# A new order of the prologue of a butterfly FFN kernel, on all engines at once

## The reference, cut to what matters

```python
# x, ctx: (32, 512, 512) f32; 16384 tokens of 512 values
def xattn(q, k, v):                       # k = v = ctx
    r_t = 0.9 * r_{t-1} + k_t * v_t       # along the 512 steps of a batch
    return q * r_t
def ffn(x):
    h = x @ W_exp + b_exp                 # 512 -> 2048
    h = butterfly(h, up_weights)          # 11 stages of 2x2 blocks; stage s pairs i and i + 2**s
    h = gelu(h + up_bias)
    h = butterfly(h, down_weights)
    return h @ W_con + b_con + down_bias  # 2048 -> 512
x = x + xattn(layernorm(x), ctx, ctx)
x = x + ffn(layernorm(x))
```

## Time and profile before

| | us |
|---|---|
| median of three runs | 2770.97 |
| the profiled execution | 2771.06 |
| its span, first to last instruction | 2769.2 |
| first 160 us | the prologue |
| TensorE busy | 2740.1 (99%) |
| VectorE busy | 2122.9 (77%) |
| ScalarE busy | 1131.0 (41%) |
| GpSimd busy | 396.5 (14%) |

### The profile page before, as it was taken

How to read it: one execution, slowest core, us unless ns; L and a number is a source line. 1 busy time by engine, 2 the same in 40 slices (tenths; PEclk the granted TensorE clock), 3 DMA queues, 4 the chain that set the end, 5 groups by cost and what they waited for, 6 DMA issues and landing times.

```text
span 2769.2 us, 35072 instructions
## 1 busy us (share of the span) xinstructions
PE 2740.1 (99%) x12191; PEld 2260.4 (82%) x12191; DVE 2122.9 (77%) x3554; ACT 1131.0 (41%) x1715; POOL 396.5 (14%) x561
## 2 busy tenths in 40 slices
PE   8899999999999999999999999999999999999998
PEld 6778888888888888888888888888888888888887
DVE  9878787778878777787877878787787877778533
ACT  5743434334343433434343343434434343343432
POOL 4712011110201111010110101011020111102000
PEclk8999999999999999999999999999999999999999
DMA  9795765758576575856757585675857557584543
GB/s 275 266 294 152 216 191 167 228 154 240 165 204 203 168 213 155 255 163 195 201 170 223 155 239 168 190 214 162 235 152 224 185 175 223 161 243 152 182 149 99
DMA packets 292021, 540.48 MB, mean 195 GB/s; under 512 B 36918, under 2 KB 98518, under 8 KB 274950
## 3 DMA queue, kind: packets, MB, share of 16 engines
q1 hardware_dynamic: 285456, 535.77, 64.7%
q10 hardware_dynamic: 5414, 1.25, 0.3%
q0 software_dynamic: 976, 1.22, 0.2%
HBM read 445.83 MB, written 60.82 MB: 183 GB/s over the span
## 4 chain that ended last, share of the span: by engine, by line
PE 98%; ACT 1%; issue 0%; DVE 0%; DMA 0%; ACTq 0%
PE ps L1767 44%; PE ps L1788 25%; PE ps L1801 25%; PE ps L1664 1%; PE ps L1570 1%; PE ps L1642 0%; PE ps L1668 0%; ACT wcon L863 0%; PE ps L1662 0%; ACT w1r L885 0%; PE ps L1670 0%; PE ps L1868 0%; DMA wexp<-in_L_ffn_W_exp_dram 0%; PE ps L1716 0%; PE ps L1589 0%
## 5 line engine op out<-in xcount | busy, mean ns | idle before, releaser
L1767 PE MATMUL ps<-xop,w1r 128*128 128x512 f32 x5376 | 1364.1, 389 | 2.5 <-DVE xop L1296 1.6
L1767 PEld LDWEIGHTS ps<-xop,w1r 128*128 128x128 f32 x5376 | 1008.8, 188 | 212.7 <-DVE xop L1296 2.0
L1788 PE MATMUL ps<-w2r,ghi 128*128 128x512 f32 x2048 | 630.5, 389 | 0.0
L1801 PE MATMUL ps<-w2r,ghi 128*128 128x512 f32 x2032 | 625.8, 389 | 0.0
L1002 ACT ACTIVATE st<-ps 128x512 f32<-128x512 f32 x384 | 229.7, 598 | 839.9 <-PE ps L1767 839.9
L1403 DVE TENSOR_TENSOR x<-ps,x 128x512 f32<-128x512 f32 x508 | 348.6, 686 | 280.6 <-PE ps L1801 278.2
L1788 PEld LDWEIGHTS ps<-w2r,ghi 128*128 128x128 f32 x2048 | 384.4, 188 | 79.8
L1801 PEld LDWEIGHTS ps<-w2r,ghi 128*128 128x128 f32 x2032 | 381.2, 188 | 79.8 <-DVE glo L1426 0.4
L1421 DVE TENSOR_TENSOR g<-ps,st 128x512 f32<-128x512 f32 x384 | 262.9, 685 | 212.5 <-PE ps L1767 212.1
L1006 ACT ACTIVATE g<-g,gelu_bias 128x512 f32<-128x512 f32 x384 | 275.4, 717 | 362.7 <-DVE g L1421 361.6
L1426 DVE TENSOR_TENSOR glo<-g,ghi 128x512 fp32r<-128x512 f32 x510 | 347.5, 702 | 79.9 <-ACT ghi L1020 79.8
(11 more groups left out here) (174 smaller groups left out, 1701.8 us busy)
## 6 DMA issues: line engine op xcount, KB each, us to landing
w1r<-w_products SPq DMA_DIRECT2D x889, 256.0 KB, 3.3
w2r<-w_split SPq DMA_DIRECT2D x126, 1024.0 KB, 5.0
x<-in_x_dram SPq DMA_DIRECT2D x128, 256.0 KB, 7.2
raw<-kv SPq DMA_DIRECT2D x480, 64.0 KB, 2.2
out_dram<-x SPq DMA_DIRECT2D x120, 256.0 KB, 4.0
kv<-in_ctx_dram SPq DMA_DIRECT2D x64, 256.0 KB, 7.3
raw<-in_ctx_dram SPq DMA_DIRECT2D x64, 256.0 KB, 5.3
wexp<-in_L_ffn_W_exp_dram SPq DMA_DIRECT2D x4, 1024.0 KB, 10.9
```

Source lines behind the costliest of these rows:

```text
L1767: last = nc.tensor.matmul(bank[:, :], w1r[:, slot, w, c * P:(c + 1) * P], xop[:, XPOS[m], v, c, :], start=(opens and i == 0), stop=(i == l ...
L1788: last = nc.tensor.matmul(ps_ya[j][:, :], g[:, p % 2, q, j * P:(j + 1) * P], w2r[:, p % 2, kk, w, :], start=(p == 0 and kk == 0 and i == 0 ...
L1801: last = nc.tensor.matmul(ps_yb[:, :], g[:, p % 2, q, j * P:(j + 1) * P], w2r[:, p % 2, kk, w, :], start=(kk == 0 and i == 0), stop=(kk == ...
```

## The change

It reorders the prologue on all five engines. Nothing after the first `product` is changed.

Loads: the two `PARTED` up stages are now loaded by SyncE, ahead of W_exp; the 15 small up loads of the high stages come ahead of the context rows; the last quarter of W_exp comes behind the context rows. The second half of x is loaded after `Z`, the second half of the context beside the `low_up` stores; `Z` comes back in five parts.

The rest of the diff, cut:

```diff
@@ fold steps
-                        last = nc.tensor.matmul(o, LX[:, 1, 4 * i + c, :], rank_major(ident[:, :]), start=True, stop=True)
+                        last = nc.tensor.transpose(o, LX[:, 1, 4 * i + c, :], ident[:, :])
-                return LX[:, 1, 4 * i:4 * i + 4, :].rearrange("p a b -> p (a b)"), whole
+                return LX[:, 1, 4 * i:4 * i + 4, :].rearrange("p a (r e) -> p a r e", e=E),\
+                    whole.rearrange("p (a e r) -> p a r e", a=4, e=E)
+                if kind == "bias_low":
+                    wait_kept(pe, "bcol", 0)
+                    for k in range(KH):
+                        last = nc.tensor.matmul(bank[:, k:k + 1], LX[:, 0, k, :], bcol[:, k:k + 1], start=True, stop=True)
@@ TensorE, high_dn
-            pe.wait_ge(bcol_kept, 1)
-            for k in range(KH):
-                last = nc.tensor.matmul(ps[4][:, 256 + k:257 + k], LX[:, 0, k, :], bcol[:, k:k + 1], start=True, stop=True)
                 fold_step("high_dn", r)
+                if r == 3:
+                    fold_step("bias_low", 0)
@@ TensorE, behind the tokens
-            pe.wait_ge(low_matrix_ready, 2)
-            for q in range(KH // 4):
-                fold_step("turn_low", q)
@@ ScalarE
+            for lane in (0, Q):
+                act.activation(sel_parts[lane:lane + Q], part_choice[0:Q], ACT.Copy).then_inc(sel_rounded, 1)
+            for stage in PARTED:
+                coefs_hi(0, stage)
+            for k in range(3):
+                fold_step("WT", k)
+            top_hi(0)
+            act.wait_ge(top_sel_ready, 2)
+            for lane in (0, Q):
+                act.activation(top_sel[lane:lane + Q], top_choice[0:Q], ACT.Copy).then_inc(top_sel_ready, 1)
+            for k in range(3, 8):
+                fold_step("WT", k)
+            coefs_hi(1, PARTED[0])
+            for k in range(8, 12):
                 fold_step("WT", k)
             for k in range(KH):
                 fold_step("low_up", k)
+                if k in WT_LAST:
+                    fold_step("WT", WT_LAST[k])
                 if k == 1:
+                    coefs_hi(1, PARTED[1])
+                if k == 3:
                     square(0, 0)
             top_hi(1)
-            act.wait_ge(path_product, UP_DONE)
-            act.wait_ge(mask_ready, 1)
-            for e in range(E):
-                last = act.activation(HX[:, 0, :, :]...)          # line 931
+            square(0, 1)
...
             for q in range(R // 4):
                 fold_step("turn_high", q)
+            for q in range(KH // 4):
+                fold_step("turn_low", q)
             weights_hi(0)
@@ VectorE
             lane_rows(0)
             coefs_lo(0)
             low_products(0)              # top_lo(0) now inside, ahead of stage 4
             top_products(0)
+            (the memsets of decay and keep, and the sum same_e)
             lane_rows(1)
             coefs_lo(1)
-            for j in range(J):
-                scan_chunk(0, 0, j)
-            stats1(0, 0, xs[0], range(J))
-            high_products(0)
+            scan_chunk(0, 0, 0)
+            scan_chunk(0, 0, 1)
+            high_products(0)
+            scan_chunk(0, 0, 2)
+            stats1(0, 0, xs[0], range(J))
+            scan_chunk(0, 0, 3)
+            gate(0, 0, xs[0], 0)
+            gate(0, 0, xs[0], 1)
+            low_products(1)
+            high_products(1)
+            top_lo(1)
+            gate(0, 0, xs[0], 2)
+            gate(0, 0, xs[0], 3)
+            top_products(1)
             dve.wait_ge(mean1_ready, J)
             stats1(0, 1, xs[0], range(J), means=False)
-            for j in range(J):
-                gate(0, 0, xs[0], j)
             means1(1)
-            top_lo(1)
-            low_products(1)
-            high_products(1)
             for j in range(J):
                 normalise(0, 0, xs[0], j)
-            top_products(1)
             scan_chunk(1, 1, 0)
             scan_chunk(1, 1, 1)
+            weights_lo(0)
             scan_chunk(1, 1, 2)
-            weights_lo(0)
             weights_lo(1)
@@ GpSimd
+            high_matrix(0)
+            pool.wait_ge(fold_made, fold_at("low_up", 11) + 1)
+            nc.gpsimd.memset(top_parts[1].bitcast(f32), 0.0).then_inc(top_zeroed, 1)
             rstd_rows(0)
-            rstd_gated(0)
+            rstd_gated(0, (0, 1))
+            high_matrix(1)
+            rstd_gated(0, (2, 3))
             rstd_rows(1)
-            pool.wait_ge(xn_ready, J)
-            high_matrix(1)
```

More of the change, by code:

```diff
@@ L250, in xattn_ffn_program @@
         up_stored = sem("up_stored")
-        z_loaded = [sem(f"z_loaded{q}") for q in range(4)]
+        z_loaded = [sem(f"z_loaded{q}") for q in range(len(Z_PARTS) - 1)]
         w1_hi = sem("w1_hi")
@@ L318, in xattn_ffn_program @@
         FOLD += [("tokens", i, "act") for i in range(2, J)]
-        FOLD += [("turn_low", q, "act") for q in range(KH // 4)]
         FOLD += [("back", k, "act") for k in range(10)]
@@ L404, in kept @@
             if kind == "low_up":
-                return low_folded[:, i, :], whole
+                return Z[:, i, :], whole
+            if kind == "bcol":
+                return bcol, whole[:, 0:2 * KH]
+            if kind == "bias_low":
+                return yb, whole[:, 0:KH]
             if kind == "high_up":
@@ L952, in _ @@
             weights_hi(1)
-            for r in range(3, 8):
+            fold_step("high_dn", 3)
+            fold_step("bias_low", 0)
+            for r in range(4, 8):
                 fold_step("high_dn", r)
@@ L959, in _ @@
             fold_step("high_dn", 12)
+            for group in range(2):
+                act.wait_ge(w1_stored[0][group], NX)
             for i in range(2):
@@ L1120, in path_products @@
                     bank, col = places[stage]
+                    if stage == PARTED[0] and not dn and not first:
+                        top_lo(0)
                     dve.wait_ge(coef_spread, spread_count(dn, first + max(stage, PARTED[0] - 1)))
@@ L1644, in fold_step @@
                     return
+                if kind == "bcol":
+                    pe.wait_ge(bias_rows_loaded, 2 * NX)
+                    nc.tensor.transpose(bank[:, 0:2 * KH], bias_rows, ident[0:2 * KH, 0:2 * KH]).then_inc(fold_made, 1)
+                    return
+                if kind == "bias_low":
+                    wait_kept(pe, "bcol", 0)
+                    for k in range(KH):
+                        last = nc.tensor.matmul(bank[:, k:k + 1], LX[:, 0, k, :], bcol[:, k:k + 1], start=True, stop=True)
+                    last.then_inc(fold_made, 1)
+                    return
                 if kind == "low_dn":
@@ L1713, in _ @@
                 fold_step("turn_high", q)
-            pe.wait_ge(bcol_kept, 1)
-            for k in range(KH):
-                last = nc.tensor.matmul(ps[4][:, 256 + k:257 + k], LX[:, 0, k, :], bcol[:, k:k + 1], start=True, stop=True)
-            last.then_inc(bias_low, 1)
+            pe.wait_ge(low_matrix_ready, 2)
+            for q in range(KH // 4):
+                fold_step("turn_low", q)
             for r in range(R):
@@ L1727, in _ @@
                 fold_step("tokens", i)
-            pe.wait_ge(low_matrix_ready, 2)
-            for q in range(KH // 4):
-                fold_step("turn_low", q)
-            pe.wait_ge(yb_kept, 1)
             wait_kept(pe, "high_dn", R - 2)
```

153 lines of the change are left out of this document (66 added, 87 removed).

## The result

The change makes the kernel slower: 2780.0 us (seven runs, 2779.22 to 2782.3) against 2771.44 us (seven runs, 2770.18 to 2772.96), a ratio of 1.0033 with a 95% interval of 1.0023 to 1.0044. The forecast was 2768.3 with a range to 2775. The profiled execution took 2779.54 us. Its span is 2777.7 us, 8.5 more than the earlier trace rows, and the page names the same bound as before.

A forecast was written before the change was run, and what follows sets the result against it. TensorE bounds the kernel (98% of the last chain), so only the prologue can pay, its end set by VectorE's queue. Scan unmoved, a 2.8 us gap gone: 2771.06 - 2.8 = 2768.3 us; own range 2766 to 2770.5, with rivals 2762 to 2775.

The forecast's parts named there:

- The path: End of the prologue: VectorE's queue sets the token split's start through the staging stores; split 2.8 us earlier.
- part 4: VectorE's queue up to the second scan: 6.0 us earlier start, 6.5 us of new gaps, scan at 73.0 us as before.
- part 1: Prologue up to low_up: TensorE gains 6 us at full clock, low_up at 22.0 instead of 28.07 us.
- The idle transposes: 32 transposes at the start, hidden under loads and memsets; at most 6.5 us on TensorE if not hidden.
- Part 2: low_up to high_up: gain spent; spreads and 16 idle products 13.1 us at full clock, high_up at 56.3 us.
- Part 3: high_up to high_dn: TensorE gains 6 us again; steps and top spreads end at 72.8 us, before 77.8.
- 0 to +0.8 us: Cost to VectorE of the up matrix expansion running on GpSimd beside a scan.
- three new gaps: VectorE waits before second coefs_lo 2.6, first scan 0.6, high_products(0) 3.3 us; 6.5 us in all.
- my gain of 1.3 us: Down top products, 4.00 us beside GpSimd's expansion, now apart from it: 0 to -1.3 us.
- The gap of 2.81 us: VectorE's wait for weights_hi(1) after the second scan goes; weights_lo(6) and all behind come 2.8 us earlier.
- B: Rival: half clock from about 45 us, high_up at 63.7 us, time +2.5 to +5.5, 2775 us; chance 0.13.
- A: Rival: early start carried through, second scan at 68.4 us, end 7.4 us earlier, 2763.7 us; chance 0.27.

The follow-up runs named there:

- e4: The changed kernel without the 32 transposes of the identity at its start; 2782.51 us, ratio 1.004 to the kernel before.
- e3: The changed kernel without the 16 idle products between the down spreads; 2782.14 us, ratio 1.0039 to the kernel before.
- e12: The changed kernel with expansions apart, no idle products, plain low_up stage, earlier load of x's second half, both coefs_hi(1) ahead of WT 8; 2773.62 us.
- e8: The kernel before with only the up high matrix expansion moved from ScalarE to GpSimd; 2771.93 us, ratio 1.0003.
- e2: The changed kernel with the up expansion back on ScalarE and GpSimd's down expansion behind all four gates; 2779.59 us, ratio 1.0029 to the kernel before.
- e1: The changed kernel with the up high matrix expansion back on ScalarE instead of GpSimd; 2782.32 us, ratio 1.0039 to the kernel before.
- e6: The changed kernel with up expansion on ScalarE, down expansion behind the gates, and no 16 idle products; 2775.6 us, ratio 1.0017 to the kernel before.
- e13: As e12, but down spreads in the old order (PARTED behind high_up 3, top behind 9); 2778.75 us, ratio 1.0025 to the kernel before.

## Why the prediction was wrong

**The path held, the terms of its ledger did not.** I had said that the end of the prologue hangs on VectorE's queue, through the stores and the token split. The last column of the table above bears that out. What failed is part 4's sum: the scan of the second half came at 84.87 us instead of 73.0, 3.8 us of it from the start that part 1 gave it, 0.5 from gaps, and 7.6 from three groups of VectorE instructions that took longer beside GpSimd.

**The term that failed first is the clock in part 1.** I wrote "from there TensorE has, at full clock"; it had half clock from 11.8 to 22.0 us. The same PLAIN took 3.09 us (the sum has 2.6, where its own working gives 4.2 - 1.8 = 2.4), PARTED 2.91 (1.6), twelve transposes 2.27 (some 1.5). 0.75 us of the delay is the start, 9.25 us for 8.5. `low_up` started at 27.04, not 22.0: 5.0 of the 6.0 us that the whole plan was to carry forward. The idle transposes, which I called free, are free (e4), and don't hold the clock: behind them TensorE stood 2.34 us and then made 16x16 products.

**Part 2's idle products are mis-sized and the effect they were bought for is missing.** Spreads and idle products took 17.25 us (49.00 to 66.25) for my 13.1; the 16 products alone 1.20 + 2.07 + 1.18 + 2.07 = 6.5 for my 3.6. Without them the same stretch is 11.5 us (e3). The rest of TensorE's chain: `low_up` 22.0 us (21.2 forecast), `high_up` with the top spreads 17.8 (16.5). Sum 5.0 + 0.8 + 4.1 + 1.3 = 11.2 us, and `turn_high` came at 84.08 for 72.8. Part 3 set that 72.8 beside "before 77.8"; 77.8 is the end of `turn_high` in the kernel before. It began at 75.99, so what the forecast gains up to there is 3.2 us, not 5.

**Part 4's "0 to +0.8 us" is 3.0 us, and 4.6 us more stand in no term.** From `lane_rows(1)` to the scan VectorE took 59.2 us (25.70 to 84.87). My 45.1 less the old gap of 0.6, the three new gaps of 2.74 + 0.57 + 3.70 = 7.0 (6.5 forecast, each where I put it), and three lengthened rows make it up: 16 columns 3.00, gate 3.36, the first copies 1.93 - 0.68 = 1.25 us. The copies' extra is the length of GpSimd's bias sum beside them; e12, where they start at 24.05, ahead of it, has them at 0.72 us. In e12 the instruction that then lies beside the bias sum, the second `coefs_lo(1)` at 26.26, takes 3.95 us for 2.28: the cost moved, it didn't go. The down expansion, for which I had only a gain, is the largest of the three: the change puts it beside a gate. Its former neighbour, the top products, took 3.88 us alone for 4.00 beside it: my gain of 1.3 us there didn't come. So the expansion was not what made them long; that their strided operand does is likely, but no run changes it.

The Trainium skill (SBUF — State Buffer, on the shared port pair) states that a GpSimd instruction that reads SBUF and a VectorE instruction with two SBUF inputs exclude each other for a whole instruction. The trace agrees (3.19 against 0.19 us; e8: 2.13 against 0.73, the one-operand statistics untouched; the one-operand copies at 25.70 are not of that kind, and no trace here shows what held them). I had applied it to the row I wanted to go away, not to the rows that would come beside the moved instruction.

**The sum went along one chain.** I added VectorE's ledger and gave TensorE's a glance. Against the forecast they came out 11.9 and 11.2 us late, against the kernel before 11.9 and 8.1. In the changed kernel VectorE's own terms make up its delay, and TensorE's doesn't reach it: e3 takes 5.8 us off TensorE and leaves VectorE's 57.8 us as they were. The second chain is right behind, though: e2 takes 6.4 us of lock-outs away, and 2.5 us arrive at the scan. So e1, e2 and e3 found nothing in the time, and e6 found 4.4 us. A price for the loss taken from one of them alone would have been wrong.

**What held.** The gap of 2.81 us before `weights_lo(1)` went, and from the scan to `weights_lo(6)` it took 47.8 us (84.87 to 132.64) for 50.5: minus 2.7, forecast 2.8. In the other kernels with the new tail the same stretch took 47.7 to 49.1 us, so the gain is 1.4 to 2.8 us. `bias_low` took 3.63 us (3.5), the `turn_low` copies 2.12 us for four. 11.9 - 2.7 = 9.2 us is what `weights_lo(6)` is late; 8.5 reached the span.

**The rivals.** B had the sign, the place and its point of decision: half clock, `high_up` more than 2 us later than 56.6, slower from 5 us on; `high_up` at 63.7 forecast, 66.25 measured. Its price (2.5 to 5.5) was too low and its way another: VectorE was not held by top spreads or `weights_hi(0)`, it came later than both. A, the early start carried through, needed the full clock that part 1 did not get.

**What stays open.** e12 leaves 2 us over the kernel before, within what the runs can tell. The steps e6 to e12 (2775.6 to 2773.62) are each smaller than the intervals of about 2.5 us either way, and only their direction is seen. No run has the changed kernel with full clock ahead of `low_up`, so what part 1's failure alone cost the time is not shown.

## What to carry to other kernels

When an instruction of GpSimd with a long run is moved, list what VectorE has beside it at the new place, and charge each first instruction with two SBUF operands with the rest of GpSimd's length. When a change starts everything earlier, add up each engine's chain to the same milestone and compare the sums: if two come out near each other, no saving on one of them counts alone, and an experiment that undoes one cause will say "no effect" of a real one. Find, too, a distance that is the same in every profile (here from the token split to the end): it names the chain that the end follows. Read an edit's effect between two milestones behind the noisy part, not from one absolute time. Price filler at the lower clock until a trace shows that it holds the higher one.

## What the runs showed of the hardware that I had not expected

- The granted clock was 0.50 in stretches where TensorE was busy throughout: 4.00 of 4.00 us with spreads and 128x512 idle products between them, 13.00 of 13.00 us in `high_dn`, whose matmuls are 128x128 (e3). Kernels with the same instructions up to there began `low_up` at 29.23 and 33.53 us (e12, e13). One profile of a prologue is thus uncertain by some us, and one absolute milestone in it can't decide between causes 2 us apart.
- A 16-column instruction took 3.19 us, and the page called it busy. Idle time alone would have hidden it; the mean of the shape shows it (0.19 us otherwise).
- The wait can fall on GpSimd as well: its down expansion took 4.76 us instead of 3.72, with VectorE's `top_lo` (67.20, 1.22 us, two SBUF operands) running at its start; 1.17 us of that were still to run when it began.
